# A graph-attention and mixture-of-experts layer: the experts' first product with its weights stationary, fetched per tile

## The chip, the cores and the metric

The kernel runs on one core of one Trainium2 chip. The metric is the device time of one execution in microseconds (us). Three executions of the kernel before took 1750.05, 1750.25 and 1754.41 us; the median is 1750.25 us.

## The reference

`x` holds 8192 tokens of 128 float32 values, `adj` an 8192 x 8192 int32 adjacency matrix. The layer is two residual steps:

```python
x = x + gnn(layernorm(x), adj, W, b_W, a_vec, b_a)      # masked attention over the graph
x = x + ffn(layernorm(x)[None], gate_w, gate_b, w1, w2, w3)[0]

def ffn(x, ...):                                         # 16 experts, hidden width 256
    top_probs, top_idx = top_k(softmax(x @ gate_w + gate_b), 2)      # then normalised to sum 1
    h1 = einsum('bsd,edh->bseh', x, w1); h2 = einsum('bsd,edh->bseh', x, w2)
    expert_out = einsum('bseh,eho->bseo', silu(h1) * h2, w3)
    return einsum('bseo,bse->bso', expert_out, dispatch)
```

The first step needs all 8192 x 8192 scores. In the second each token goes to two of 16 experts, so 16384 rows pass through a product 128 to 512 (w1 and w2 side by side), silu times gate, and a product 256 to 128.

## The kernel before

**Graph attention, 0 to about 1409 us.** Nine blocks of target rows (4 or 8 tiles of 128 rows) run over 64 tiles of source rows each. The SP queue streams the adjacency matrix into a ring of five staging buffers (`load_half`, L418 to L425), each load waiting for ScalarE's `sign` to have used the buffer. TensorE turns masks (L975) and accumulates the attention product (L990), VectorE makes logits (L1270), ScalarE exponentials (L779). While a block runs, the block before is normalised and routed, and GpSimd scatters its rows by indirect DMA to `xd_d`, a table in DRAM sorted by expert (`scatter`, L622 to L636: eight scatters for the first choice, a wait until all of them have landed, an iota on L619, eight for the second choice).

**Between the stages.** The last block is normalised and routed alone, a table `tab` of 144 tiles (first row and expert of each) is made, and the last rows are scattered. All of `w1` and `w2` (4 MB) has been loaded into one SBUF tile `w12` during the last block (L449 to L452).

**Experts, about 1436 to 1708 us.** 144 tiles of 128 rows, all of one expert each. I call the work of TensorE between two `m_h` a step. For tile i:

- SP loads the 128 rows, 130 words each (`load_tile`, L459 to L462), into `xs`, eight slots. The load of tile i waits on `y_out` until the result of tile i-8 has been written (L483), because its slot holds that tile's destinations and gate weight.
- `t_x` (L1063): TensorE transposes the rows into PSUM; ScalarE copies them to `xsT` (L871).
- `m_h` (L1067): one product with the rows as stationary operand and the expert's 512 columns of `w12` as moving operand. The expert's number is a register, read from `tab` by `expert_of` (L1058).
- ScalarE makes silu (L877), VectorE multiplies with the gate half (`do_hid`, L1527).
- `t_h` (L1073): two transposes of the 256 hidden columns; VectorE copies them to `hidT` (`copy_hT`, L1534).
- `m_y` (L1080): two accumulating products with `w3s`; ScalarE copies with the gate weight as scale (L883) into `ys`, four slots.
- GpSimd scatters the tile to `res_d` by indirect DMA (L698 to L702), which signals `y_out` when it lands.

TensorE's order is written out by hand: in step i come `m_h(i)`, `expert_of(i+1)`, `t_x(i+1)`, `t_h(i-1)`, `m_y(i-2)` (L1094 to L1128), with the first and the last eight tiles unrolled and a hardware loop of eight tiles in between. SP has a loop of eight tiles too (L480 to L484), at whose head one instruction loads eight registers of row numbers (`rows_of`). A float32 product of 128 rows is issued as two instructions, each with its own weight load (LDWEIGHTS); a transpose is one.

After the first eight row loads SP issues one load of 4 MB, `xm` (L479), for the last stage, which gathers the two results of every token, adds and stores (L487 to L496, L1545 to L1553).

Of the kernel before, what the change touches and what calls it, by code (L numbers as in the profile page):

```python
# [16 lines left out]
P = 128  # L17
# [23 lines left out]
def graph_moe_layer(nc, x, adj, W, b_W, a_vec, b_a, gate_w, gate_b, w1, w2, w3, out):  # L41
# [21 lines left out]
    SU = 4  # L63
    XS = 8
    GR = 8

# [38 lines left out]
    s1_d = nc.dram_tensor("s1_d", (NT, P), F32, kind="Internal").ap()  # L105
    xd_d = nc.dram_tensor("xd_d", (E * CAP + E * P, RW), F32, kind="Internal").ap()
    res_d = nc.dram_tensor("res_d", (2 * N + 2 * E * P, D), F32, kind="Internal").ap()

    with ExitStack() as ctx:
# [3 lines left out]
        def sem(name):  # L113
            return ctx.enter_context(nc.semaphore(name))
# [130 lines left out]
        xm, _ = carve(rA, 0, NT, D)  # L245
        w12, _ = carve(rB, 0, E, 2 * HID)
        w3s, _ = carve(urow[:, :].bitcast(F32), 0, E, HC * D)
# [5 lines left out]
        silu, at = carve(prf, at, 2, HID)  # L253
        hid, at = carve(prf, at, 2, HID)
        xsT, at = carve(prf, at, 2, D)
        hidT, at = carve(prf, at, 2, HID)
        ys, at = carve(prf, at, SU, D)
# [112 lines left out]
        tchain = sem("tchain")  # L370
        xs_in = [sem(f"xs_in{i}") for i in range(XS)]
        xsT_done = sem("xsT_done")
# [4 lines left out]
        hT_done = sem("hT_done")  # L377
        hT_ready = sem("hT_ready")
        y_done = sem("y_done")
# [34 lines left out]
        def _(sp):  # L414
# [3 lines left out]
            def load_half(b, i):  # L418
                c, k = pieces(b)[i // 2]
                n = 2 * PIECE0[b] + i  # L420
                if n >= STG:
                    sp.wait_ge(sign_done, n - STG + 1)
                r = (ROW0[b] + k) * P
                at = c * CH + i % 2 * HC2
                sp.dma_start(stage[:, n % STG, :], adj[r:r + P, at:at + HC2]).then_inc(adj_in[n % STG], 16)  # L425

            def load_s1(b):
# [30 lines left out]

            def load_tile(u, r, done):  # L459
                if done:  # L460
                    sp.wait_ge(y_out[u % SU], 16 * done)
# [7 lines left out]
            sp.wait_ge(tab_ready, 1)  # L469
            r = rows_of(0, XS)  # L470
            for c in range(2):
                sp.wait_ge(disp[c], 16 * NT)
            sp.wait_ge(pad_out, 16 * E)
            for u in range(XS):
                load_tile(u, r[u], 0)
            sp.wait_ge(xmid_out, 16 * LAST)
# [433 lines left out]
        def _(pe):  # L910
# [162 lines left out]
            def t_h(i, u):  # L1073
                pe.wait_ge(hid_ready, i + 1)
                for c in range(HC):
                    t = pe.transpose(bank[4 + u % 2][:, c * P:(c + 1) * P], hid[:, u % 2, c * P:(c + 1) * P],  # L1076
                                     identf[:, :])
                t.then_inc(hT_done, 1)

            def m_y(i, u, e, first):  # L1080
                pe.wait_ge(hT_ready, i + 1)
                if not first:
                    pe.wait_ge(y_ready, i - 1)
                for c in range(HC):
                    m = pe.matmul(bank[6 + u % 2][:, 0:D], hidT[:, u % 2, c * P:(c + 1) * P],  # L1085
                                  w3s[:, bass.ds(e, 1), c * D:(c + 1) * D].rearrange("p a b -> p (a b)"),
                                  start=(c == 0), stop=(c == HC - 1))
                m.then_inc(y_done, 1)


            pe.wait_ge(w12_in, 32)
            e = {0: expert_of(0)}
            t_x(0, 0, 1)
            for i in range(XS):  # L1094
                m_h(i, i, e[i])
                if i + 1 < XS:
                    e[i + 1] = expert_of(i + 1)
                t_x(i + 1, (i + 1) % XS, (i + 1) // XS + 1)
                if i >= 1:
                    t_h(i - 1, i - 1)  # L1100
                if i >= 2:
                    m_y(i - 2, i - 2, e[i - 2], i - 2 < 2)
            with pe.Fori(1, ST // XS - 1) as g:
                e = {0: expert_of(XS * g)}
# [11 lines left out]
            e = {first: expert_of(first)}  # L1116
            for i in range(first, ST + 2):
                if i < ST:
                    m_h(i, i % XS, e[i])
                    if i - 2 < first:  # L1120
                        e[i - 2] = expert_of(i - 2)
                    if i + 1 < ST:
                        e[i + 1] = expert_of(i + 1)
                if i + 1 < ST:
                    t_x(i + 1, (i + 1) % XS, (i + 1) // XS + 1)
                if i - 1 < ST:
                    t_h(i - 1, (i - 1) % XS)
                m_y(i - 2, (i - 2) % XS, e[i - 2], False)  # L1128

        @block.vector  # L1130
        def _(dve):
# [390 lines left out]

            def do_hid(i, v, first):
                dve.wait_ge(silu_ready, i + 1)
                if not first:
                    dve.wait_ge(hT_done, i - 1)
# [3 lines left out]
            def copy_hT(i, v, first):  # L1530
                dve.wait_ge(hT_done, i + 1)
                if not first:
                    dve.wait_ge(y_done, i - 1)
                dve.tensor_copy(hidT[:, v, :], bank[4 + v][:, 0:HID]).then_inc(hT_ready, 1)  # L1534

            do_hid(0, 0, True)
            copy_hT(0, 0, True)
            do_hid(1, 1, True)
            copy_hT(1, 1, True)
            with dve.Fori(1, ST // 2) as g:  # L1540
                for v in range(2):
                    do_hid(2 * g + v, v, False)
                    copy_hT(2 * g + v, v, False)

# [30 lines left out]
```

## Time and profile before

| | us |
|---|---|
| median of the three executions | 1750.25 |
| the profiled execution, own time | 1744.61 |
| its span | 1742.8 |
| experts' stage, first row load issued to last scatter | 1435.9 to 1705.2 |
| TensorE busy in the span | 1524.1 (87%) |
| VectorE, ScalarE, GpSimd busy | 1429.4, 1330.3, 495.5 |

Times in rows are microseconds from the start of the span. A timeline row gives start, duration, engine, line, instruction, tiles, count, and in brackets how long the engine was idle before it and what it waited for. PEld is TensorE's weight load, PEldq and SPq are the instruction streams of TensorE and SyncE, POOL is GpSimd, DVE VectorE and ACT ScalarE. A row "x4" merges four instructions: its start is the first one's start, its duration reaches to the end of the last.

### The profile page before, as it was taken

What the parts mean: (1) busy time and instruction counts of PE and PEld (TensorE: products, weight loads), DVE (VectorE), ACT (ScalarE), POOL (GpSimd) and SP (SyncE); (2) the same over time, 40 slices, a digit from 0 to 9 for tenths busy, and PEclk for the clock granted to TensorE, in tenths of its full rate; (3) what the DMA queues carried; (4) which work ended last, traced back from release to release, by engine and by line L of the source; (5) the groups of instructions that cost most, each with busy time, mean ns of one, the idle gap of its engine ahead of it and who ended that gap; (6) DMA issues with size and microseconds to landing.
All of it is one profiled execution on the core that took longest, in us unless ns stands there. A gap on an engine that the chain in (4) does not pass through costs nothing.

```text
span 1742.8 us, 24899 instructions
## 1 busy us (share of the span) xinstructions
PE 1524.1 (87%) x8110; PEld 837.4 (48%) x8111; DVE 1429.4 (82%) x1896; ACT 1330.3 (76%) x1804; POOL 495.5 (28%) x716
## 2 busy tenths in 40 slices
PE   5687899899989989998999899989999939999991
PEld 5554354454444444444444444445554515666660
DVE  6899999989998998999899989997895743444444
ACT  4899899889979987998798889977785624545550
POOL 6500001120314032403411260313025254555551
PEclk9999999999999999999999999999999979999996
DMA  7889687648847774886488657845523334222227
GB/s 244 298 303 316 219 283 251 218 160 262 258 145 245 236 261 136 261 256 233 139 268 259 203 175 260 265 139 159 157 73 104 111 69 159 72 71 73 75 73 298
DMA packets 127715, 339.40 MB, mean 195 GB/s; under 512 B 16962, under 2 KB 48898, under 8 KB 127490
## 3 DMA queue, kind: packets, MB, share of 16 engines
q1 hardware_dynamic: 106208, 304.06, 54.1%
q0 software_dynamic: 17056, 27.17, 5.8%
q10 hardware_dynamic: 4354, 6.92, 1.2%
q8 instruction: 56, 0.92, 0.2%
q14 instruction: 41, 0.34, 0.1%
HBM read 309.57 MB, written 28.51 MB: 194 GB/s over the span
## 4 chain that ended last, share of the span: by engine, by line
PE 39%; DVE 37%; issue 17%; ACT 3%; DMA 3%; POOL 2%; another core or an unknown queue 0%; SPq 0%; ACTq 0%; DVEq 0%; POOLq 0%
PE pair L990 18%; DVE probs L1270 17%; DVE ring L1238 16%; PE pair L1069 8%; PE pair L975 5%; PE pair L1085 4%; PE pair L1076 2%; ACT ring L728 1%; POOL X L536 1%; DMA ring<-res_d 1%; PE pair L1065 1%; DVE part L1238 1%; ACT probs L779 1%; PE pair L935 1%; DMA res_d<-probs 1%
## 5 line engine op out<-in xcount | busy, mean ns | idle before, releaser
L990 PE MATMUL pair<-probs,X 128*128 128x512 f32 x2048 | 1010.7, 611 | 1.9 <-ACT probs L779 1.8
L779 ACT ACTIVATE probs<-probs,ebias 128x1024 f32<-128x1024 f32 (+1 forms) x576 | 601.0, 1046 | 185.8 <-DVE probs L1270 179.4
L1270 DVE SCALAR_TENSOR_TENSOR probs<-s1row,ns,pair 128x1024 f32<-128x1024 f32 (+1 forms) x576 | 653.9, 1157 | 85.5 <-PE pair L975 73.0
L1238 DVE CUSTOM_DVE_ANT_0 ring<-urow,ring 128x2048 int8<-128x2048 f16 x256 | 585.0, 2289 | 5.7 <-ACT urow L747 4.9
L728 ACT ACTIVATE ring<-stage,neghalf 128x1024 int8<-128x1024 int32 x512 | 574.3, 1138 | 0.0
L975 PEld LDWEIGHTS pair<-diag,ring 128*128 128x128 fp8e5 x4096 | 262.4, 99 | 461.5 <-DVE probs L1270 258.2
L990 PEld LDWEIGHTS pair<-probs,X 128*128 128x128 f32 x2048 | 346.1, 192 | 219.3 <-issue 215.1
L975 PE MATMUL pair<-diag,ring 128*128 128x128 bf16 x4096 | 326.6, 220 | 117.2 <-DVE probs L1270 101.5
L700 POOL DMA_INDIRECT res_d<-probs x144 | 139.6, 969 | 133.6 <-ACT probs L883 125.7
L1534 DVE COPY probs<-pair 128x256 f32<-128x256 f32 x144 | 61.2, 425 | 139.6 <-PE pair L1076 89.6
L634 POOL DMA_INDIRECT xd_d<-xres,sloti x120 | 154.6, 1288 | 38.6 <-issue 31.6
L1069 PE MATMUL pair<-ring,probs 128*128 x288 | 158.6, 633 | 7.4 <-issue 4.1
L871 ACT ACTIVATE probs<-pair 128x128 f32<-128x128 f32 x144 | 40.0, 278 | 126.3 <-PE pair L1065 106.9
L576 POOL DMA_DIRECT2D xres<-in_x x7 | 11.7, 1672 | 358.6 <-ACT xres L821 358.6
L553 POOL TENSOR_SCALAR mrow<-rmax,kS,kB 128x8 f32<-128x8 f32 (+1 forms) x9 | 3.1, 350 | 379.4 <-DVE rmax L1246 379.4
L1085 PE MATMUL pair<-urow,probs 128*128 x576 | 89.1, 277 | 0.1
L1527 DVE TENSOR_TENSOR probs<-probs,pair 128x256 f32<-128x256 f32 x144 | 60.7, 421 | 19.0 <-ACT probs L877 15.8
L1085 PEld LDWEIGHTS pair<-urow,probs 128*128 128x128 f32 x576 | 75.6, 191 | 1.0 <-issue 0.3
L883 ACT ACTIVATE probs<-pair,probs 128x128 f32<-128x128 f32 x144 | 53.1, 369 | 23.1 <-PE pair L1085 6.9
L1076 PE MATMUL pair<-identf,probs 128*128 128x128 f32 x288 | 55.3, 274 | 0.4 <-ACT probs L883 0.4
L877 ACT ACTIVATE probs<-pair 128x256 f32<-128x256 f32 x144 | 54.4, 378 | 0.6 <-PE pair L1069 0.6
L1065 PE MATMUL pair<-identf,probs 128*128 128x128 f32 x144 | 41.1, 286 | 13.1 <-DMA probs<-xd_d 12.5
(239 smaller groups left out, 768.8 us busy)
## 6 DMA issues: line engine op xcount, KB each, us to landing
stage<-in_adj SPq DMA_DIRECT2D x512, 512.0 KB
probs<-xd_d SPq DMA_DIRECT2D x144, 65.0 KB
ring<-res_d SPq DMA_DIRECT2D x16, 512.0 KB, 9.8
ring<-in_L_ffn_w SPq DMA_DIRECT2D x2, 2048.0 KB, 11.8
ring<-xmid_d SPq DMA_DIRECT2D x1, 4096.0 KB
out<-ring ACTq DMA_DIRECT2D x8, 512.0 KB, 7.0
s1row<-s_d SPq DMA_DIRECT2D x7, 512.0 KB, 6.4
xres<-in_x POOLq DMA_DIRECT2D x7, 512.0 KB, 14.1
```

Source lines behind the costliest of these rows:

```text
L634: pool.indirect_dma_start(out=xd_d[:, :], out_offset=bass.IndirectOffsetOnAxis(ap=sloti[:, q, c, k:k + 1], axis=0), in_=xres[:, q, k, :], ...
L700: pool.indirect_dma_start(out=res_d[:, :], out_offset=bass.IndirectOffsetOnAxis(ap=xsI[:, i % XS, D:D + 1], axis=0), in_=ys[:, i % SU, :], ...
L728: act.activation(mask(b, c, k)[:, h:h + HC2], stage[:, n % STG, :], ACT.Sign, bias=neghalf[:, 0:1], scale=1.0).then_inc(sign_done, 1)
L779: act.activation(probs[:, n % PR, 0:wide], probs[:, n % PR, 0:wide], ACT.Exp, bias=ebias[:, j:j + 1], scale=RISE).then_inc(probs_ready, 1)
L975: t = pe.matmul(Tp[n % 2][:, k * P:(k + 1) * P], mask8(b, j, k), diag[:, q, k, :], start=True, stop=True)
L990: m = pe.matmul(acc[q][:, lo:hi], X[:, j, :], probs[:, n % PR, lo:hi], start=(j == 0), stop=(j == NT - 1))
L1069: pe.matmul(bank[2 + u % 2], xsT[:, u % 2, :], w12[:, bass.ds(e, 1), :].rearrange("p a b -> p (a b)"), start=True, stop=True).then_inc(h_d ...
L1076: t = pe.transpose(bank[4 + u % 2][:, c * P:(c + 1) * P], hid[:, u % 2, c * P:(c + 1) * P], identf[:, :])
L1085: m = pe.matmul(bank[6 + u % 2][:, 0:D], hidT[:, u % 2, c * P:(c + 1) * P], w3s[:, bass.ds(e, 1), c * D:(c + 1) * D].rearrange("p a b -> p ...
L1238: dve.tensor_tensor_reduce(m, urow[:, c * CH:(c + 1) * CH], m, CODE, NO_EDGE, ALU.subtract, ALU.max, part[:, k, c:c + 1]).then_inc(piece_d ...
L1270: dve.scalar_tensor_tensor(out=probs[:, n % PR, 0:wide], in0=s1row[:, q, 0:wide], scalar=ns2[:, j:j + 1], in1=Tp[n % 2][:, 0:wide], op0=AL ...
L1534: dve.tensor_copy(hidT[:, v, :], bank[4 + v][:, 0:HID]).then_inc(hT_ready, 1)
```

## The change

The first product of the experts is turned round: the weights are the stationary operand, in four blocks of 128 columns, and the transposed rows are the moving one, so the hidden values come out transposed. `t_h`, `copy_hT`, the tile `hid` and two semaphores go; `do_hid` writes `hidT` directly, which has four slots instead of two. `w12` no longer lies in SBUF as a whole: `w1` and `w2` are copied side by side into a DRAM tensor `w12_d` by 32 DRAM to DRAM transfers of 128 KB, issued by SP in blocks 2 to 5, and for each tile SP fetches its expert's 256 KB into one of eight slots `wt`. TensorE transposes rows two tiles ahead, so that step i is `m_h(i)`, `expert_of(i-1)`, `t_x(i+2)`, `m_y(i-2)`. The core of the diff:

```diff
+        wt, _ = carve(rB, 0, WS, 2 * HID)
-            sp.wait_ge(trans_done, used_up(GALL - 3))
-            w12v = w12.rearrange("p e (k h) -> p e k h", k=2)
-            sp.dma_start(w12v[:, :, 0, :], w1.rearrange("e d h -> d e h")).then_inc(w12_in, 16)
-            sp.dma_start(w12v[:, :, 1, :], w2.rearrange("e d h -> d e h")).then_inc(w12_in, 16)
+            def pair_weights(n):
+                e, k = divmod(n, 2)
+                sp.dma_start(w12_d[e, :, k * HID:(k + 1) * HID], (w1, w2)[k][e, :, :]).then_inc(w12_in, 16)
...
+                    if 2 <= b < 6 and i % 8 == 4:
+                        pair_weights(8 * (b - 2) + i // 8)
...
+            def load_weights(u, e):
+                sp.dma_start(wt[:, u, :], w12_d[bass.ds(e, 1), :, :].rearrange("a d h -> d (a h)")
+                             ).then_inc(wt_in[u], 16)
...
             for u in range(XS):
-                load_tile(u, r[u], 0)
+                load_tile(u, r[u])
+                load_weights(u, e[u])
...
             with sp.Fori(1, ST // XS) as g:
                 r = rows_of(XS * g, XS)
+                e = experts_of(XS * g, XS)
                 for u in range(XS):
+                    sp.wait_ge(h_done, XS * g + (u - XS + 1))
+                    load_weights(u, e[u])
                     sp.wait_ge(y_out[u % SU], 32 * g + (16 * (u // SU) - 16))
-                    load_tile(u, r[u], 0)
+                    load_tile(u, r[u])
...
-            def m_h(i, u, e):
+            def m_h(i, u, w, uses):
                 pe.wait_ge(xsT_ready, i + 1)
-                pe.matmul(bank[2 + u % 2], xsT[:, u % 2, :],
-                          w12[:, bass.ds(e, 1), :].rearrange("p a b -> p (a b)"), start=True, stop=True
-                          ).then_inc(h_done, 1)
+                pe.wait_ge(wt_in[w], 16 * uses)
+                for c in range(2 * HC):
+                    m = pe.matmul(bank[2 + u % 2][:, c * P:(c + 1) * P], wt[:, w, c * P:(c + 1) * P], xsT[:, u % 2, :],
+                                  start=True, stop=True)
+                m.then_inc(h_done, 1)
...
+            def free_h(i):
+                pe.wait_ge(hid_ready, i - 1)
...
                 for u in range(XS):
                     i = XS * g + u
-                    m_h(i, u, e[u])
-                    if u < 2:
-                        e[u - 2] = expert_of(XS * g + (u - 2))
-                    if u + 1 < XS:
-                        e[u + 1] = expert_of(XS * g + (u + 1))
-                    t_x(i + 1, (u + 1) % XS, g + 1 if u + 1 < XS else g + 2)
-                    t_h(i - 1, (u - 1) % XS)
+                    free_h(i)
+                    m_h(i, u, u, g + 1)
+                    if u == 0:
+                        e[-2] = expert_of(XS * g + -2)
+                    e[u - 1] = expert_of(XS * g + (u - 1))
+                    t_x(i + 2, (u + 2) % XS, g + 1 if u + 2 < XS else g + 2)
                     m_y(i - 2, (u - 2) % XS, e[u - 2], False)
...
-                dve.tensor_tensor(hid[:, v, :], silu[:, v, :], bank[2 + v][:, HID:2 * HID], ALU.mult
+                    dve.wait_ge(y_done, i - (HB - 1))
+                dve.tensor_tensor(hidT[:, w, :], silu[:, v, :], bank[2 + v][:, HID:2 * HID], ALU.mult
                                   ).then_inc(hid_ready, 1)
```

## Rows read from the trace of the kernel before

**Rows 1.** The page, its chain that ended last, shares of the span by line

```profile
PE pair L990 18%; DVE probs L1270 17%; DVE ring L1238 16%; PE pair L1069 8%; PE pair L975 5%; PE pair L1085 4%; PE pair L1076 2%; ACT ring L728 1%; POOL X L536 1%; DMA ring<-res_d 1%; PE pair L1065 1%; DVE part L1238 1%; ACT probs L779 1%; PE pair L935 1%; DMA res_d<-probs 1%
```

**Rows 2.** By stretch: length, busy PE, PEld, DVE, ACT, POOL; clock, DMA share, GB/s

```profile
1370.00:1374.00 4.00, 4.00 (x24) 2.17 (x23) 2.44 (x5) 2.66 (x4) 3.35 (x11) 1.00 1.10 359
1448.00:1452.00 4.00, 4.00 (x24) 2.94 (x23) 2.13 (x6) 2.33 (x9) 2.41 (x3) 1.00 0.97 412
...
1600.00:1640.00 40.00, 39.00 (x204) 25.50 (x203) 17.99 (x45) 20.50 (x68) 21.64 (x23) 1.00 0.27 73
```

**Rows 3.** Timeline of TensorE, one step of the experts' stage

```profile
1446.65 1.09 PE L1069 MATMUL pair<-ring,probs 128*128 x2
1447.58 0.27 PE L1065 MATMUL pair<-identf,probs 128*128 128x128 f32 x1
1447.69 0.38 PE L1076 MATMUL pair<-identf,probs 128*128 128x128 f32 x2
1447.90 0.61 PE L1085 MATMUL pair<-urow,probs 128*128 x4
1448.35 1.09 PE L1069 MATMUL pair<-ring,probs 128*128 x2
```

**Rows 4.** Timeline of TensorE, `m_h` of tile 8 and of tile 143, the last

```profile
1457.15 1.12 PE L1069 MATMUL pair<-ring,probs 128*128 x2
...
1700.52 1.09 PE L1069 MATMUL pair<-ring,probs 128*128 x2
```

**Rows 5.** TensorE's instruction stream by line, 1590 to 1633: ns min/median/max

```profile
L1059 PEldq TENSOR_LOAD <-stage x30: 295/300/429, 1590.4 to 1632.1; - x30
L1083 PEldq EVENT_SEMAPHORE  x18: 51/51/51, 1592.6 to 1630.0; - x18
```

**Rows 6.** Timeline of TensorE, eight pairs of weight load and matmul, then the next

```profile
800.84 0.62 PE L975 MATMUL pair<-diag,ring 128*128 128x128 bf16 x8
801.30 1.94 PE L990 MATMUL pair<-probs,X 128*128 128x512 f32 x4
```

**Rows 7.** Timeline: scatters on GpSimd, row loads on SP, around loop heads

```profile
1449.20 0.97 POOL L700 DMA_INDIRECT res_d<-probs  x1 [0.73 <-ACT probs L883]
1605.66 0.98 POOL L700 DMA_INDIRECT res_d<-probs  x1 [1.63 <-ACT probs L883]
...
1595.31 0.33 SPq L462 DMA_DIRECT2D probs<-xd_d  x1
1597.07 0.33 SPq L462 DMA_DIRECT2D probs<-xd_d  x1
1608.06 0.33 SPq L462 DMA_DIRECT2D probs<-xd_d  x1
```

**Rows 8.** SP's instruction stream, 1590 to 1640, one load of eight registers: ns, first start

```profile
L455 SPq TENSOR_LOAD <-stage x4: 558/572/595, 1596.0 to 1639.1; - x4
```

**Rows 9.** Timeline of the stage's start: SP's issues, and `t_x` of tile 8

```profile
1435.87 4.37 SPq L462 DMA_DIRECT2D probs<-xd_d  x8
1440.36 0.36 SPq L479 DMA_DIRECT2D ring<-xmid_d  x1
1454.15 6.27 SPq L462 DMA_DIRECT2D probs<-xd_d  x6
1456.01 0.33 PE L1065 MATMUL pair<-identf,probs 128*128 128x128 f32 x1 [1.48 <-DMA probs<-xd_d]
```

**Rows 10.** Timeline in a block: 512 KB loads, last scatter, iota that waits for it

```profile
853.60 0.33 SPq L425 DMA_DIRECT2D stage<-in_adj  x1
854.63 0.33 SPq L425 DMA_DIRECT2D stage<-in_adj  x1
...
854.83 0.96 POOL L634 DMA_INDIRECT xd_d<-xres,sloti  x1 [0.30 <-issue]
859.26 0.15 POOL L619 IOTA xres<- 128x8 int32 x1 [3.47 <-DMA xd_d<-xres,sloti]
```

**Rows 11.** The page, costliest groups: busy, mean ns, then idle before

```profile
L728 ACT ACTIVATE ring<-stage,neghalf 128x1024 int8<-128x1024 int32 x512 | 574.3, 1138 | 0.0
```

More of the change, by code:

```diff
@@ L64, in graph_moe_layer @@
     XS = 8
+    WS = 8
+    HB = 4
     GR = 8
@@ L106, in graph_moe_layer @@
     xd_d = nc.dram_tensor("xd_d", (E * CAP + E * P, RW), F32, kind="Internal").ap()
+    w12_d = nc.dram_tensor("w12_d", (E, D, 2 * HID), F32, kind="Internal").ap()
     res_d = nc.dram_tensor("res_d", (2 * N + 2 * E * P, D), F32, kind="Internal").ap()
@@ L245, in graph_moe_layer @@
         xm, _ = carve(rA, 0, NT, D)
-        w12, _ = carve(rB, 0, E, 2 * HID)
+        wt, _ = carve(rB, 0, WS, 2 * HID)
         w3s, _ = carve(urow[:, :].bitcast(F32), 0, E, HC * D)
@@ L253, in graph_moe_layer @@
         silu, at = carve(prf, at, 2, HID)
-        hid, at = carve(prf, at, 2, HID)
         xsT, at = carve(prf, at, 2, D)
-        hidT, at = carve(prf, at, 2, HID)
+        hidT, at = carve(prf, at, HB, HID)
         ys, at = carve(prf, at, SU, D)
@@ L371, in graph_moe_layer @@
         xs_in = [sem(f"xs_in{i}") for i in range(XS)]
+        wt_in = [sem(f"wt_in{i}") for i in range(WS)]
         xsT_done = sem("xsT_done")
@@ L376, in graph_moe_layer @@
         hid_ready = sem("hid_ready")
-        hT_done = sem("hT_done")
-        hT_ready = sem("hT_ready")
         y_done = sem("y_done")
@@ L457, in rows_of, with experts_of, load_tile @@
                     skip_runtime_bounds_check_because="the first row of a tile in an expert's part of the dispatch")[1]
-            def load_tile(u, r, done):
-                if done:
-                    sp.wait_ge(y_out[u % SU], 16 * done)
+            def experts_of(i, n):
+                return nc.values_load_multi_w_load_instructions(
+                    tab[0:1, bass.ds(ST + i, n)], engines=(mybir.EngineType.SP,), min_val=0, max_val=E - 1,
+                    skip_runtime_bounds_check_because="every tile of the table belongs to one of the experts")[1]
+            def load_tile(u, r):
                 sp.dma_start(xs[:, u, :], xd_d[bass.ds(r, P), :]).then_inc(xs_in[u], 16)
+            def load_weights(u, e):
+                sp.dma_start(wt[:, u, :], w12_d[bass.ds(e, 1), :, :].rearrange("a d h -> d (a h)")
+                             ).then_inc(wt_in[u], 16)
             sp.wait_ge(proj_read, ROUND0[NB])
@@ L470, in _ @@
             r = rows_of(0, XS)
+            e = experts_of(0, XS)
             for c in range(2):
@@ L473, in _ @@
             sp.wait_ge(pad_out, 16 * E)
+            sp.wait_ge(w12_in, 16 * 2 * E)
             for u in range(XS):
-                load_tile(u, r[u], 0)
+                load_tile(u, r[u])
+                load_weights(u, e[u])
             sp.wait_ge(xmid_out, 16 * LAST)
@@ L1065, in t_x, with m_y @@
                 pe.transpose(bank[u % 2][:, 0:P], xs[:, u, 0:D], identf[:, :]).then_inc(xsT_done, 1)
-            def m_h(i, u, e):
+            def m_h(i, u, w, uses):
                 pe.wait_ge(xsT_ready, i + 1)
-                pe.matmul(bank[2 + u % 2], xsT[:, u % 2, :],
-                          w12[:, bass.ds(e, 1), :].rearrange("p a b -> p (a b)"), start=True, stop=True
-                          ).then_inc(h_done, 1)
-            def t_h(i, u):
-                pe.wait_ge(hid_ready, i + 1)
[L1075 to L1081, printed above, removed]
+                pe.wait_ge(wt_in[w], 16 * uses)
[3 more added lines that the diff above has]
+                m.then_inc(h_done, 1)
+            def m_y(i, u, e, first):
+                pe.wait_ge(hid_ready, i + 1)
                 if not first:
@@ L1084, in m_y @@
                 for c in range(HC):
-                    m = pe.matmul(bank[6 + u % 2][:, 0:D], hidT[:, u % 2, c * P:(c + 1) * P],
+                    m = pe.matmul(bank[6 + u % 2][:, 0:D], hidT[:, u % HB, c * P:(c + 1) * P],
                                   w3s[:, bass.ds(e, 1), c * D:(c + 1) * D].rearrange("p a b -> p (a b)"),
@@ L1088, in m_y @@
                 m.then_inc(y_done, 1)
-            pe.wait_ge(w12_in, 32)
-            e = {0: expert_of(0)}
+            def free_h(i):
+                pe.wait_ge(hid_ready, i - 1)
+            e = {}
             t_x(0, 0, 1)
+            t_x(1, 1, 1)
             for i in range(XS):
[L1095 to L1098, printed above, removed]
+                if i >= 2:
+                    free_h(i)
+                m_h(i, i, i, 1)
                 if i >= 1:
-                    t_h(i - 1, i - 1)
+                    e[i - 1] = expert_of(i - 1)
+                t_x(i + 2, (i + 2) % XS, (i + 2) // XS + 1)
                 if i >= 2:
@@ L1103, in _ @@
             with pe.Fori(1, ST // XS - 1) as g:
-                e = {0: expert_of(XS * g)}
+                e = {}
                 for u in range(XS):
                     i = XS * g + u
-                    m_h(i, u, e[u])
-                    if u < 2:
-                        e[u - 2] = expert_of(XS * g + (u - 2))
-                    if u + 1 < XS:
-                        e[u + 1] = expert_of(XS * g + (u + 1))
-                    t_x(i + 1, (u + 1) % XS, g + 1 if u + 1 < XS else g + 2)
-                    t_h(i - 1, (u - 1) % XS)
+                    free_h(i)
+                    m_h(i, u, u, g + 1)
[3 more added lines that the diff above has]
+                    t_x(i + 2, (u + 2) % XS, g + 1 if u + 2 < XS else g + 2)
                     m_y(i - 2, (u - 2) % XS, e[u - 2], False)
             first = ST - XS
-            e = {first: expert_of(first)}
+            e = {}
             for i in range(first, ST + 2):
                 if i < ST:
[L1119 to L1125, printed above, removed]
+                    free_h(i)
+                    m_h(i, i % XS, i % WS, i // WS + 1)
+                if i == first:
+                    e[i - 2] = expert_of(i - 2)
                 if i - 1 < ST:
-                    t_h(i - 1, (i - 1) % XS)
+                    e[i - 1] = expert_of(i - 1)
+                if i + 2 < ST:
+                    t_x(i + 2, (i + 2) % XS, (i + 2) // XS + 1)
                 m_y(i - 2, (i - 2) % XS, e[i - 2], False)
@@ L1521, in _, with do_hid @@
             dve.tensor_copy(tab[0:1, :], bank[3][0:1, 0:2 * ST]).then_inc(tab_ready, 1)
-            def do_hid(i, v, first):
+            def do_hid(i, v, w, first):
                 dve.wait_ge(silu_ready, i + 1)
                 if not first:
-                    dve.wait_ge(hT_done, i - 1)
-                dve.tensor_tensor(hid[:, v, :], silu[:, v, :], bank[2 + v][:, HID:2 * HID], ALU.mult
+                    dve.wait_ge(y_done, i - (HB - 1))
+                dve.tensor_tensor(hidT[:, w, :], silu[:, v, :], bank[2 + v][:, HID:2 * HID], ALU.mult
                                   ).then_inc(hid_ready, 1)
[L1530 to L1543, printed above, removed]
+            for i in range(HB):
+                do_hid(i, i % 2, i, True)
+            with dve.Fori(1, ST // HB) as g:
+                for w in range(HB):
+                    do_hid(HB * g + w, w % 2, w, False)
             dve.wait_ge(xm_in, 16)
```

## The prediction

> **What bounds the kernel now.** I read the chain that ended last first: beside the attention's lines it holds L1069, L1085, L1076 and L1065, together 15% of the span [rows 1]. They are TensorE's products and transposes of the experts' stage, the part that the change rewrites. The busy times by stretch come second: in that stage TensorE is busy 39.0 of 40 us at the full clock (2.4 GHz), VectorE 18.0, ScalarE 20.5, GpSimd 21.6, and the DMA engines have a share of 0.27 [rows 2]. So the stage runs at TensorE's pace. The timeline gives the step: `m_h` 0.93 us, `t_x` 0.11, the two of `t_h` 0.21, `m_y` 0.45, in all 1.70 [rows 3]. From `m_h` of tile 8 to that of tile 143 it is 243.4 us, 1.803 for each of 135 steps [rows 4]; eight take 14.4, of which 0.8 is the head of the hardware loop.
>
> **TensorE's part.** A pair of a weight load and a 128-column matmul is passed every 0.11 us (`m_y`: four in 0.45; `t_h`: two in 0.21) [rows 3]. The new `m_h` is four blocks of two such pairs: 8 x 0.1125 = 0.90 for 0.93, so turning the product round costs nothing, and `t_h` is gone. The new step is 13 pairs, 1.46 us. The instruction stream has to keep up: 26 instructions at no more than 0.029 (eight pairs in 0.46 [rows 6]) are 0.75, the register load of `expert_of` 0.30, and six waits and three register operations, all taken like the wait of 0.051 [rows 5], 0.45. That is 1.50, and I take it; the bounds are 1.46 and 1.56. At the loop head I keep 0.8; its lower bound is 0.5, one register load less. TensorE alone would go at (8 x 1.50 + 0.8) / 8 = 1.60.
>
> Here a rule speaks against the change. The trace shows four pairs on `m_y` in 0.45 us, each with a weight load of its own [rows 3], so loads pass beside the matmul before. The Trainium skill (TensorE: Matmul & The Clock Gate, The mechanism) says that a weight load overlaps a running matmul only if it goes to another row group, which full 128-row loads never do; by it no load would be hidden.
>
> **What the removed work was worth elsewhere.** `copy_hT` leaves VectorE, which was idle half the time: nothing. The load of `w12` ran while TensorE was busy 4.00 of 4.00 us [rows 2]: nothing. The 32 copies in DRAM come between adjacency loads for which ScalarE never sat idle [rows 11]: nothing; with that cover gone it would be 8 MB of traffic at 359 GB/s [rows 2], 23 us. `free_h` waits for a product that VectorE ends some 1 us after its `m_h`, two steps ahead: nothing. The weights of tile i are issued before its rows and used two steps after `t_x(i)`, and 256 KB at 412 GB/s [rows 2] are 0.64 us: never late.
>
> **The loop that was slack.** The rows of tile j+8 are loaded once the scatter of tile j has landed. From such a load's issue to the transpose is 1.86 us (1454.15 to 1456.01 [rows 9]); from `m_y` to the scatter's start 1.30 (1447.90 to 1449.20 [rows 3, 7]); from there to SP's next load 2.40 (1605.66 to 1608.06 [rows 7]). Before, `t_x(j+8)` comes five steps after `m_y(j)`: with `t_x` and `t_h` between, 5.88 us against 8.5, nobody waits. Now it comes four steps after: 0.11 + 1.30 + 2.40 + 1.86 = 5.67 against 4 x 1.50 = 6.0. The slack is nearly gone, by the transpose moved one tile ahead and by the shorter step.
>
> And SP becomes late once in eight tiles. Its registers for eight tiles load 0.7 us after the last row load of the group was issued and take 0.57 [rows 7, 8]; now a second such load follows (0.6), then the weights' issue (0.56, as eight issues and the next took 4.49 [rows 9]), and about 0.1 of waits and registers on either side: the row load of tile 8g comes 2.55 us after that of 8g-1, where a step is 1.5. So there is a closed chain from one group to the next: rows of 8g land 1.86; three steps of TensorE over the loop head 3 x 1.50 + 0.8 = 5.3; `t_x`, `m_y`, scatter, landing 3.81, which releases the rows of 8g+7; SP to the rows of 8g+8 2.55. The sum is 13.52 for eight tiles, more than TensorE's 12.8: 1.69 a step.
>
> **Contention.** The trace has no stage with scatters beside 256 KB bursts, so I bound it. Below: nothing. Above, the nearest row: in a block two loads of 512 KB were issued around a scatter, and it landed after 4.43 us for 2.40 [rows 10, 7], 2.0 us late, where the 1 MB takes 2.6 at 404 to 412 GB/s: a scatter loses at most what the bytes beside it take. That is 0.64 for the scatter and 0.64 for the rows behind the weights in SP's queue, 1.3 in the chain. In steady order the bursts mostly fall between the scatters, and SP issues the two 0.56 apart; I take 0.5. The chain is 14.02, 1.753 a step, and 135 steps are 236.6: 6.8 us less.
>
> The Trainium skill (DMA: Bandwidth & Descriptors, Latency and other measured facts) gives the memory 0.2 us of latency on average and 2 at high load. By that the two transfers in the chain could be 3.6 longer, an estimate from that page, and the kernel would take about 1801.
>
> **The start.** SP issues the 4 MB `xm` after the first loads, and the scatter of tile 0 lands only once `xm` is through; then tile 8 is loaded, at 1454.15 [rows 9]. Eight more issues put `xm` 8 x 0.56 = 4.5 us later; half a weight transfer behind it adds 0.3. `t_x(8)` moves from 1456.0 to 1460.8. It now belongs to step 6, so `m_y` and one whole step follow: 0.11 + 0.45 + 1.50, `m_h(8)` at 1462.9 for 1457.15: 5.7 us more. Bounds: 3.5 and 8. After the last `m_h` nothing of weight changes.
>
> **Sum.** -6.8 + 5.7 = -1.1 us. The profiled execution took 1744.61 (span 1742.8), 5.6 under the median of 1750.25; so it would take 1743.5, and the median 1749.2.
>
> **The rivals.**
>
> Faster: the chain through SP does not close. The two register loads overlap (0.6 less) and the bursts miss the scatters (0.2 left): 13.1 for eight tiles, 1.64 a step, 22.0 less, and with the start 16.3 less: 1734. For it: nothing reads the second eight registers before the weights' issue, and before the change the head of SP's loop was hidden. Against it: a register load takes 0.57 and SP's stream is in order. It decides under 13.78 us per eight tiles.
>
> Slower: every burst delays the next scatter and the next rows by its whole 0.64. The chain is 14.8, 1.853 a step, 6.7 more, with the start 12.4 more: 1763. For it: the loaded scatter lost three quarters of the time of the bytes beside it [rows 10], and 256 KB more each step put the DMA share at 0.28 + 0.64 / 1.8, about 0.65. It decides above 14.4 us, a contention of 0.9. At the top of the start's bound it would be 1765, with a step of 1.56 on TensorE 1768.
>
> The turned product is not cheap: no weight load is hidden. A load is 25.5 us for 203 [rows 2], 0.13 each, so a step is 13 x (0.13 + 0.11) = 3.1 us, 175 more: 1931. That is what the rule on row groups would do; the rows of `m_y` refute it unless more than four pairs in a row differ.
>
> **Chances.** 0.3% of 1750 is 5.3 us, about what a measurement can tell. The chain as I price it, 13.78 to 14.4: 0.38, its own range 1744.9 to 1755.5. Faster: 0.33, most of it in 1733 to 1745. Slower: 0.28, to 1768. Exposed weight loads: 0.01. The range of 1733 to 1768 leaves out about 2 in 10 (a chain under 13.1; contention above 1.3).
>
> **What would show it.** In the changed profile: `m_h` starts to `t_x` 0.9 us with eight matmuls; TensorE idle before L1065 (`t_x`) for DMA, about 1 us once in eight tiles; SP's row load of 8g some 2.5 us after the one before; scatter start to SP's next row load 2.4 to 3.0; a step of 1.75 on average; `m_h(8)` near 1463; VectorE some 60 us less busy; the DMA share 0.6 to 0.7. The prediction is wrong if TensorE is idle before `t_x` in every step (contention), if it never is (the chain does not close), or if ScalarE now sits idle before L728.

## The result and the profile after

The changed kernel takes 1781.65 us (1776.60 to 1782.63, four runs) where the kernel before takes 1750.15 (medians). The ratio of the mean times is 1.0168, with a 95% interval of 1.0143 to 1.0194. It is slower by 31 us, outside the range of the prediction. The profiled execution has a span of 1779.0 us for 1742.8.

The busy times by stretch (columns as in [rows 2]), first the attention stage of the kernel before, then the changed kernel:

```profile
0.00:1400.00 1400.00, 1257.03 (x6765) 666.27 (x6767) 1275.61 (x1515) 1189.24 (x1357) 338.11 (x552) 1.00 0.68 215
...
0.00:1400.00 1400.00, 1256.32 (x6771) 666.84 (x6773) 1275.91 (x1516) 1189.91 (x1357) 331.45 (x553) 1.00 0.68 215
...
1560.00:1600.00 40.00, 34.63 (x259) 30.65 (x259) 8.38 (x20) 18.43 (x60) 19.47 (x21) 1.00 0.70 198
1600.00:1640.00 40.00, 35.02 (x263) 30.85 (x262) 8.25 (x21) 18.44 (x60) 19.15 (x20) 1.00 0.68 196
```

TensorE is now busy 35.0 of 40 us where it was 39.0 [rows 2], and the DMA share went from 0.27 to 0.68. The attention stage did not move: its busy times are those of before within 7 us (GpSimd) and 1 us (the others), ScalarE still never waits for an adjacency load (idle before L746, the `sign`, is 0.0 us, as in [rows 11]), and the experts' first row load is issued at 1436.54 for 1435.87. The page's rows of `t_x`, before and after (busy, mean ns, then idle before it), show TensorE waiting for rows:

```profile
L1065 PE MATMUL pair<-identf,probs 128*128 128x128 f32 x144 | 41.1, 286 | 13.1 <-DMA probs<-xd_d 12.5
L1083 PE MATMUL pair<-identf,probs 128*128 128x128 f32 x144 | 45.7, 317 | 58.2 <-DMA probs<-xd_d 49.3
```

What stopped TensorE stands in its timeline, here with SP's issues and GpSimd's scatters (L1083 is `t_x`, L1090 `m_h`, L1099 `m_y`, L718 the scatter, L470 SP's row load, L473 its weight load; other rows are left out):

```profile
1601.43 0.33 PE L1083 MATMUL pair<-identf,probs 128*128 128x128 f32 x1
1602.17 1.06 PE L1090 MATMUL pair<-probs,ring 128*128 128x128 f32 x8
1603.02 0.97 POOL L718 DMA_INDIRECT res_d<-probs  x1 [0.98 <-ACT probs L901]
1603.07 0.27 PE L1083 MATMUL pair<-identf,probs 128*128 128x128 f32 x1
1603.16 0.33 SPq L470 DMA_DIRECT2D probs<-xd_d  x1
1603.62 1.06 PE L1090 MATMUL pair<-probs,ring 128*128 128x128 f32 x8
1605.40 0.33 PE L1083 MATMUL pair<-identf,probs 128*128 128x128 f32 x1 [0.73 <-DMA probs<-xd_d]
1606.15 1.06 PE L1090 MATMUL pair<-probs,ring 128*128 128x128 f32 x8
1606.20 0.33 SPq L470 DMA_DIRECT2D probs<-xd_d  x1
```

Where nothing stops it, a step is 1.45 us (`m_h` at 1602.17 and 1603.62), but 115 of the 119 steps from `t_x` to `t_x` up to tile 142 are longer than 1.5. Here the row load issued at 1603.16 lands for a `t_x` at 1605.40, 2.24 us later, and TensorE stood idle for it. The scatter of 1603.02 releases the row load of 1606.20, 3.18 us later. From `m_h` of tile 8 (1464.22) to that of tile 143 (1735.37) it is 271.2 us, 2.01 a step, for 1.80 before [rows 4].

The chain that ended last says the same by line, first before (1460 to 1690), then after (1480 to 1700):

```profile
by line: PE pair L1069 52.2%; PE pair L1085 24.7%; PE pair L1076 12.0%; PE pair L1065 8.8%; issue 2.2%; ACT probs L871 0.2%
...
by line: DMA res_d<-probs 22.5%; DMA probs<-xd_d 21.1%; issue 17.5%; PE pair L1090 9.7%; PE pair L1099 8.9%; SPq L470 4.6%; PE pair L1083 4.5%; SPq L473 4.3%; ACT probs L901 2.6%; SPq L465 1.6%; SPq L460 1.1%; SPq L495 0.6%; POOL res_d L718
```

Before, the chain was TensorE's products. Now its first two lines are the scatter to DRAM and the rows from there. I call them the two ways: the scatter's way runs from a scatter's start to the row load that it releases, the rows' way from a row load to its `t_x`. I took both for each of 120 tiles (row loads of tiles 24 to 143) from the starts in the timeline. The scatter's way has a median of 3.52 us, least 2.59, the rows' way 2.90, least 1.86. The quiet values, against which I count contention below, are the prediction's 2.40 and 1.86. For the scatter's way the trace before has a median of 2.42. For the rows' way it has no median to compare, since there the rows mostly lie ready before TensorE wants them: 1.86 is the one load for which `t_x` waited [rows 9]. SP was already waiting when the scatter landed for 97 of the 120 row loads, so the scatter's way is in the main DMA and not SP's lateness.

### The profile page after: what moved, and what is told of

Read it like the earlier page. It is cut to its first block, busy times and chain, and to the rows that moved or that the text cites. A ratio compares the mean times of both kernels' runs of the same rounds, so it can differ in the third digit from the quotient of the medians.

```text
span 1779.0 us, 26224 instructions
## 1 busy us (share of the span) xinstructions
PE 1518.1 (85%) x8686; PEld 895.0 (50%) x8687; DVE 1372.6 (77%) x1752; ACT 1330.5 (75%) x1804; POOL 487.4 (27%) x716
## 4 chain that ended last, share of the span: by engine, by line
DVE 36%; PE 29%; issue 19%; DMA 10%; SPq 2%; POOL 2%; ACT 1%; ACTq 0%; another core or an unknown queue 0%; POOLq 0%; DVEq 0%
PE pair L1008 18%; DVE probs L1286 17%; DVE ring L1254 16%; PE pair L993 5%; DMA res_d<-probs 4%; DMA probs<-xd_d 4%; PE pair L1090 2%; PE pair L1099 2%; POOL X L554 1%; DMA ring<-res_d 1%; PE pair L1083 1%; DVE part L1254 1%; SPq L470 1%; SPq L473 1%; PE pair L953 1%
## 5 line engine op out<-in xcount | busy, mean ns | idle before, releaser
L746 ACT ACTIVATE ring<-stage,neghalf 128x1024 int8<-128x1024 int32 x512 | 574.2, 1138 | 0.0
L718 POOL DMA_INDIRECT res_d<-probs x144 | 139.2, 966 | 171.1 <-ACT probs L901 157.9
L1090 PE MATMUL pair<-probs,ring 128*128 128x128 f32 x1152 | 156.0, 279 | 1.8 <-issue 0.2
L652 POOL DMA_INDIRECT xd_d<-xres,sloti x120 | 146.2, 1218 | 38.7 <-issue 31.7
L1090 PEld LDWEIGHTS pair<-probs,ring 128*128 128x128 f32 x1152 | 142.4, 194 | 4.8 <-issue 4.5
L1099 PE MATMUL pair<-urow,probs 128*128 x576 | 98.7, 294 | 1.5 <-ACT probs L901 1.5
L1083 PE MATMUL pair<-identf,probs 128*128 128x128 f32 x144 | 45.7, 317 | 58.2 <-DMA probs<-xd_d 49.3
L1099 PEld LDWEIGHTS pair<-urow,probs 128*128 128x128 f32 x576 | 75.5, 191 | 8.5 <-issue 1.6
L1083 PEld LDWEIGHTS pair<-identf,probs 128*128 128x128 f32 x144 | 20.4, 142 | 77.4 <-DMA probs<-xd_d 52.2
```

Source lines behind the costliest of these rows:

```text
L652: pool.indirect_dma_start(out=xd_d[:, :], out_offset=bass.IndirectOffsetOnAxis(ap=sloti[:, q, c, k:k + 1], axis=0), in_=xres[:, q, k, :], ...
L718: pool.indirect_dma_start(out=res_d[:, :], out_offset=bass.IndirectOffsetOnAxis(ap=xsI[:, i % XS, D:D + 1], axis=0), in_=ys[:, i % SU, :], ...
L746: act.activation(mask(b, c, k)[:, h:h + HC2], stage[:, n % STG, :], ACT.Sign, bias=neghalf[:, 0:1], scale=1.0).then_inc(sign_done, 1)
L1083: pe.transpose(bank[u % 2][:, 0:P], xs[:, u, 0:D], identf[:, :]).then_inc(xsT_done, 1)
L1090: m = pe.matmul(bank[2 + u % 2][:, c * P:(c + 1) * P], wt[:, w, c * P:(c + 1) * P], xsT[:, u % 2, :], start=True, stop=True)
L1099: m = pe.matmul(bank[6 + u % 2][:, 0:D], hidT[:, u % HB, c * P:(c + 1) * P], w3s[:, bass.ds(e, 1), c * D:(c + 1) * D].rearrange("p a b -> ...
```

## The experiments

The kernels of a group ran on one chip, and the kernel before ran beside them: it took 1733.22 us beside the first group, 1744.06 beside the second and 1732.24 beside the third. So all times are compared as ratios to the kernel before on the same chip. The diffs show the lines that matter; "..." stands for what is left out. "Step" is the mean distance of `t_x` from tile 24 to 142; it is 1.81 us in the kernel before and 2.02 in the changed one.

**First group: what is it?** e1 takes the traffic away:

```diff
                 for u in range(XS):
-                    sp.wait_ge(h_done, XS * g + (u - XS + 1))
-                    load_weights(u, e[u])
                     sp.wait_ge(y_out[u % SU], 32 * g + (16 * (u // SU) - 16))
...
-                    m_h(i, u, u, g + 1)
+                    m_h(i, u, u, 1)
```

> The changed kernel without the 136 weight loads inside SP's loop; the register loads of experts stay, every tile after the eighth uses the weights of the first eight tiles (the hidden values are those of wrong experts). Theory (the row loop): a row load waits for the scatter eight tiles back and is needed four steps after m_y; the loop is 5.67 us of latency plus what the weight traffic adds, about 2.2. Without the traffic 5.67 / 4 = 1.42 falls below TensorE's 1.60, so the step goes from 2.0 to about 1.6 and the kernel to about 1727. Rival A (SP's lateness at the group head carries it): the second register load stays, so no more than 0.6 us in eight tiles comes back, 10 us: about 1771. Rival B (13 pairs and their instruction stream cost more than 1.5 on TensorE): no change, 1782.

Measured: 0.9849 (0.9822 to 0.9876), 1709.6 us, step 1.56. The chip is another than the one I expected a time for; by ratio it is 56 us below the change. The computation turned round is fast; the traffic, with what waits for it and SP's work to issue it, is the whole loss. Rivals A and B fall. This run also has the quiet ways in steady work, as the median time from issue to landing; below it the same lines of g0, the changed kernel taken once more in the third group:

```profile
probs<-xd_d SPq DMA_DIRECT2D x115, 65.0 KB, 1.8
res_d<-probs POOLq DMA_INDIRECT x116, 2.3
...
probs<-xd_d SPq DMA_DIRECT2D x91, 65.0 KB, 3.0
res_d<-probs POOLq DMA_INDIRECT x91, 3.4
```

e3 keeps the traffic and gives the rows more slots:

```diff
-    XS = 8
+    XS = 16
...
-        xs, at = carve(prf, at, XS, RW)
+        xs, at = carve(rB, at, XS, RW)
...
+                    for v in range(WS):
+                        u = WS * half + v
+                        sp.wait_ge(h_done, XS * g + (u + 1))
+                        load_weights(v, e[v])
+                        sp.wait_ge(y_out[u % SU], 64 * g + (16 * (u // SU) + 16))
+                        load_tile(u, r[v])
```

> The changed kernel with sixteen slots for rows instead of eight (they move into the free half of the ring region behind the weight slots), weights still eight slots and the same traffic. Theory (row loop): the loop now spans twelve steps, so contention of 2 us in it is hidden, TensorE sets the step at about 1.6, the kernel takes 1730 to 1740. Rival (the traffic itself is the bound, through the weight transfers or the result slots): the step stays near 2.0 and the kernel near 1780.

Measured: 0.9906 (0.9878 to 0.9934), 1717.9 us, step 1.63. With the same bytes moving and the rows needed twelve steps after `m_y` instead of four, the loss turns into a gain. The waits of e3 in 1490 to 1660 show what is left (engine, line, whom it waited for, us in total, times, longest): TensorE no longer waits for rows but for weights.

```profile
PE pair L1099 <- DMA ring<-w_d: 9.0, 16, 1.4
PEld pair L1099 <- DMA ring<-w_d: 8.3, 11, 1.6
```

e4 does the traffic alone, in the kernel before:

```diff
                 for u in range(XS):
+                    sp.wait_ge(h_done, XS * g + (u - XS + 1))
+                    sp.wait_ge(dum_in[u], 16 * g + 16)
+                    sp.dma_start(dum[:, u, :], x_4[u * P:(u + 1) * P, :]).then_inc(dum_in[u], 16)
                     sp.wait_ge(y_out[u % SU], 32 * g + (16 * (u // SU) - 16))
...
```

> The kernel before with nothing changed but 136 transfers of 256 KB from DRAM to unused SBUF slots, issued by SP just where the change issues the weights. Theory (row loop): contention adds 2 us to the loop, 5.88 + 2.2 = 8.1 us against five steps of 1.70 (8.5): nearly hidden, plus SP's later issue at the group head; 1750 to 1757. Rival (the traffic costs as such, whatever the lead): about 1780 as with the change. The traces also give the contention alone: scatter start to the next row load 2.4 before, about 3.5 here.

Measured: 1.0017 (1.0003 to 1.0031), 1737.2 us, step 1.80. The contention is all there: the median of the scatter's way is 3.56 us for 2.40. It costs 3 us in the whole kernel by ratio, since the loop has five steps of 1.7.

e5 takes the change's other part back:

```diff
-                    t_x(i + 2, (u + 2) % XS, g + 1 if u + 2 < XS else g + 2)
+                    t_x(i + 1, (u + 1) % XS, g + 1 if u + 1 < XS else g + 2)
```

> The changed kernel with rows transposed one tile ahead again (t_x(i+1) in step i), all else as changed. The loop then spans five steps, 7.9 / 5 = 1.58, but each m_h has to wait for ScalarE's copy of a transpose that ended 0.45 us before: 0.3 to 0.4 of idle per step, 1.85 with the loop head. Theory (row loop): about 1760. Rival A (SP or traffic as such): 1782 or more, since nothing of theirs changed and the wait comes on top.

Measured: 0.9995 (0.9981 to 1.0009), 1732.5 us, step 1.74. One step more in the loop is worth what the change lost, though `m_h` now waits for the copy of the rows. I had priced that wait at 0.3 to 0.4 in each step; most steps are 1.64, so it is 0.2 over the undisturbed 1.45.

**Second group: do the causes add, and what sets the contention?** The two parts go into the kernel before, f3 with rows transposed two tiles ahead, f4 with that and e4's traffic:

```diff
-                    t_x(i + 1, (u + 1) % XS, g + 1 if u + 1 < XS else g + 2)
+                    t_x(i + 2, (u + 2) % XS, g + 1 if u + 2 < XS else g + 2)
```

> The kernel before with one thing changed: rows are transposed two tiles ahead (t_x(i+2) in step i), as the change does. The row loop then spans four steps of 1.70: 6.8 us for 5.88 needed. Theory (row loop): still slack, the time is that of before within 3 us. Rival (the order of TensorE's work itself costs): slower by more than 5 us.

> The kernel before with both: rows transposed two tiles ahead, and the 136 unused transfers of 256 KB. Theory (row loop): 5.88 + 2.2 = 8.1 us over four steps is 2.0 a step for 1.80: 25 to 30 us slower than before, though the traffic alone cost 3 us and the transpose ahead alone costs none. Rival (the causes add): about 3 us slower than before.

Measured: f3 0.9981 (0.9967 to 0.9995), f4 1.0161 (1.0143 to 1.0180), steps 1.74 and 1.93. With e4, which ran on the chip of the first group, this makes a table of two causes:

| kernel before, ratio | no traffic | 256 KB a tile |
|---|---|---|
| rows one tile ahead (loop of five steps) | 1 | 1.0017 |
| rows two tiles ahead (loop of four) | 0.9981 | 1.0161 |

Alone, the traffic costs 0.2% and the order gains 0.2%; both together cost nearly what the change costs (1.0168). They don't add; they meet in one loop.

f2 asks for SP's lateness at the head of its loop:

```diff
-                e = experts_of(XS * g, XS)
...
-                    load_weights(u, e[u])
+                    sp.dma_start(wt[:, u, :], w12_d[u, :, :]).then_inc(wt_in[u], 16)
```

> The changed kernel with the same weight traffic, but from fixed experts, so that SP's loop has no second load of eight registers (wrong experts' weights from tile 8 on). Theory (row loop with contention in every step): SP's row load at the group head comes 0.6 us earlier, which matters once in eight tiles: 0 to 10 us less than the change. Rival (SP's lateness at the head is what binds, as the chain of the prediction had it): the whole 0.6 per group comes back, 10 us, and the step without it falls to 1.9 or less.

Measured: 1.0158 (1.0139 to 1.0177), step 1.93. SP's row load at the head came 2.19 us after the one before (median) for 2.75 in the change, so the lateness was shortened as meant, and the stage gives back 0.06 to 0.09 a step (against g0 and the change), some 10 us, at the upper end of my expectation. By whole times it is less: 1.0158 lies within the interval of the change's own 1.0168 on the first chip and outside that of the repeat below, 1.0198 (1.0180 to 1.0216). So the second register load costs something between nothing and 12 us of the 31; these runs do not fix it better. My test did not separate theory and rival well, as both allowed 10 us; the step of 1.93 is above the 1.9 that the rival wanted.

f1 halves the bytes of each weight load, the number of descriptors stays:

```diff
+            def load_half_weights(u, e):
+                sp.dma_start(wt[:, u, 0:HID], w12_d[bass.ds(e, 1), :, 0:HID].rearrange("a d h -> d (a h)")
+                             ).then_inc(wt_in[u], 16)
...
-                    load_weights(u, e[u])
+                    load_half_weights(u, e[u])
```

> The changed kernel, but each weight load inside SP's loop brings only w1's half of an expert, 128 KB in rows of 1 KB, as many descriptors as before (the gate half of the hidden values is then that of a wrong expert). Theory A (the bytes beside a transfer delay it): the contention of about 2.2 us in the loop of four steps halves, 5.67 + 1.1 over 4 is 1.7, the step goes from 2.0 to 1.7 and the kernel loses 35 to 40 us against the change. Theory B (each transfer delays the others by a fixed time, whatever its size): the step stays at 1.95 to 2.0, within 8 us of the change.

Measured: 1.0061 (1.0044 to 1.0078), 1755.0 us, step 1.82; the scatter's way is 2.93 us, the rows' 2.29. Of the change's 1.12 and 1.04 us of contention 0.53 and 0.43 are left, a little under half. The bytes count, as A says, but the time fell less than I expected, about 19 us by ratio where I had 35 to 40. The steps tell why. Seven of eight are 1.68 us on average, as the plain loop gives (the two ways and the rest are 5.22 + 1.41 = 6.6 us, 1.66 a step). The eighth, which ends with `t_x` of a tile 8g, is 2.81: SP issues that tile's row load 3.10 us after the one before (median). The chain of the prediction through SP's head gives 13.52 + 0.96 = 14.5 us for eight tiles, 1.81 a step, which is the 1.82 measured, and SP came too late to wait for the landing in 50 of 120 row loads, for 23 in the change. So with the contention halved it is that chain that closes. In the change itself the eighth step is 2.35 and the others 1.97.

**Third group.** g0 is the changed kernel, unedited:

> The changed kernel as it is, once more on this chip, so that the three beside it can be compared with it directly: about 1.017 of the kernel before, step 2.0.

Measured: 1.0198 (1.0180 to 1.0216), 1765.8 us, step 1.99, the two ways 3.50 and 2.84: the loss is there on a second chip, and a little larger. This trace tells for 30 of the 120 tiles when their rows landed: `t_x` starts 0.04 or 0.05 us later in 24 of them and at most 0.26 later in five more, so TensorE did wait for nearly every tile.

g3 moves the same bytes as 64 rows of 4 KB:

```diff
-                    load_weights(u, e[u])
+                    sp.dma_start(wt[0:64, u, :], w12_d[bass.ds(e[u], 1), :, :].rearrange("a (d q) h -> d (a q h)", q=2)
+                                 ).then_inc(wt_in[u], 16)
```

> The changed kernel with the in-loop weight loads of the same 256 KB laid out as 64 rows of 4 KB instead of 128 of 2 KB (the weights then lie wrongly; the product of all tiles after the eighth is that of stale weights). In f1 half the bytes in the same number of descriptors halved the contention: a scatter lost 0.5 us instead of 1.1. Theory A (the bytes count): the same 2.0 a step, 1.017. Theory B (the 2 KB rows move below the full rate, and it is the time that the engines are held that counts): contention falls towards 0.64 for each transfer, 1.75 to 1.85 a step, 15 to 30 us less than the change.

Measured: 1.0347 (1.0325 to 1.0369), 1791.3 us, step 2.15, the two ways 4.02 and 3.17. Neither theory had that sign: bytes alone do not explain it. But B's quantity, the time for which the engines are held, orders the three runs. The stretches of g3 and of f1 (columns as in [rows 2]):

```profile
1520.00:1560.00 40.00, 32.20 (x238) 28.43 (x239) 7.40 (x18) 16.86 (x54) 17.47 (x19) 1.00 0.75 182
```

```profile
1520.00:1560.00 40.00, 36.76 (x286) 33.43 (x285) 9.54 (x23) 19.84 (x69) 20.42 (x22) 1.00 0.51 146
```

Share times step, less the 0.27 x 1.80 = 0.49 us that rows and results take [rows 2, 4], is the time for which one tile's weights hold all engines. It is an estimate: the shares differ by some 0.03 between stretches of one run, which is 0.1 us.

| | share x step - 0.49 | scatter's way over 2.40 | rows' way over 1.86 |
|---|---|---|---|
| f1, 128 rows of 1 KB | 0.51 x 1.82: 0.44 | 0.53 | 0.43 |
| the change, 128 of 2 KB | 0.68 x 2.01: 0.88 | 1.12 | 1.04 |
| g3, 64 of 4 KB | 0.75 x 2.15: 1.12 | 1.62 | 1.31 |

The delay goes with the time held, at 1.0 to 1.5 of it. Three points that differ in more than one thing do not prove a law, and why 64 longer rows are slower than 128 was not tried.

g1 and g2 follow the waits of e3. g1 is e3 with the load `xm` cut into pieces; g2 is g1 with SP loading rows twelve tiles ahead in its sixteen slots. The second diff is against g1:

```diff
             with sp.Fori(0, ST // XS - 1) as g:
+                sp.dma_start(xm[:, bass.ds(GR * g, GR), :], xm_src[:, bass.ds(GR * g, GR), :]).then_inc(xm_in, 16)
...
```

> Sixteen row slots (as in e3) and the 4 MB load xm cut into eight loads of 512 KB, one every sixteen tiles in SP's loop. Theory: in e3 TensorE stood still for 13 us after tile 9, because the scatter of tile 0, which the result slots wait for, lands only behind xm; with the pieces that stop goes, the pieces cost 1.3 us each of DMA time and mostly hide: 8 to 12 us less than e3's ratio of 0.9906, about 0.985. Rival (the stop has another cause, or the pieces stop the stage eight times): no better than 0.99.

```diff
                         load_weights(v, e[v])
-                        sp.wait_ge(y_out[u % SU], 64 * g + (16 * (u // SU) + 16))
-                        load_tile(u, r[v])
+                        if u >= 4 or not peeled:
+                            sp.wait_ge(y_out[u % SU], 64 * g + 16 * (u // SU))
+                        load_tile((u + 12) % XS, r[v])
```

> g1 with one more edit: SP loads rows twelve tiles ahead instead of sixteen, still in sixteen slots, so it waits for a scatter twelve tiles back, which has long landed, and issues each tile's weights as soon as their slot is free. Theory: what is left in e3 (1.63 a step against 1.56 without traffic) is TensorE waiting for weights that SP issued late, behind its wait for the scatter; it goes: 1.58 a step, 5 to 8 us less than g1. Rival (the weights come late because the DMA engines are near full): as g1.

Measured: g1 0.9921 (0.9904 to 0.9937), step 1.68; g2 0.9720 (0.9698 to 0.9742), 1684.6 us, step 1.449. g1 alone gave nothing: the stop before `t_x` of tile 10 shrank from 13.4 to 5.3 us (distance to the `t_x` before it), but the pieces of 512 KB stand before the weights in SP's queue. TensorE waited 12.5 us for weights in 1490 to 1640, and the step right behind a piece, one in sixteen, takes 3.45 us on average where e3 has 2.30. g2 then gave 33 us where I had expected 5 to 8. Its stretch:

```profile
1520.00:1560.00 40.00, 40.00 (x361) 40.00 (x361) 11.38 (x27) 25.48 (x84) 27.35 (x29) 1.00 0.95 301
```

TensorE is busy 40 of 40 us while the DMA engines are at 0.95. In all 118 steps the distance is 1.449 or 1.450. The rival, that full DMA engines make the weights late, is refuted: the engines are fuller than in g1 (0.85) and the weights come in time, so SP had issued them late. This version beats both kernels, the one before by 2.8%, 48 us.

## Why the prediction was wrong

- **The step on TensorE.** Right in kind and too careful. I had 1.46 from the pairs, and took 1.50 for the instruction stream and 0.8 for the loop head, 1.60 together. g2 shows 1.449 including its loop heads, so both additions were nothing there. The rule that a weight load overlaps only a matmul on another row group (the Trainium skill, TensorE: Matmul & The Clock Gate, The mechanism) is contradicted: thirteen pairs in a row pass at 0.11 us each, with the rows of matmuls and of weight loads both busy 40.00 of 40.00 us at a granted clock of 1.00 (2.4 GHz).
- **The work taken off VectorE, the copies in DRAM, the weights' own lateness.** Right in the changed kernel: VectorE is busy 57 us less (1429.4 to 1372.6), and TensorE had not waited for that copy before (idle before L1085, `m_y`, 0.1 us). No wait for weights stands in the traces of the change, e5, f1, f2, g0 or g3. They came late only in e3 and g1, where SP waited for other things first.
- **The start.** `t_x(8)` was forecast at 1460.8 and came at 1460.73. `m_h(8)` was forecast at 1462.9 and came at 1464.22: 7.1 us later than before, for 5.7. The 1.4 us missed are TensorE's clock. It had stood idle for 10.14 us before `t_x(8)`, and the granted clock was 0.54 from 1460 to 1464, the lower of its two levels (1.2 GHz) for most of it; `m_h(7)` took 1.89 us for 1.06:

```profile
1460.00:1464.00 4.00, 3.27 (x16) 3.25 (x17) 0.00 (x0) 0.67 (x3) 0.97 (x1) 0.54 0.80 238
1464.00:1468.00 4.00, 4.00 (x38) 4.00 (x37) 1.26 (x3) 2.09 (x8) 1.93 (x2) 1.00 0.37 114
...
1460.73 0.48 PE L1083 MATMUL pair<-identf,probs 128*128 128x128 f32 x1 [10.14 <-DMA probs<-xd_d]
1461.01 1.15 PE L1099 MATMUL pair<-urow,probs 128*128 x4
1461.95 1.89 PE L1090 MATMUL pair<-probs,ring 128*128 128x128 f32 x8
```

- **The loop without contention.** The way and its length were right: 5.67 us over four steps, slack nearly gone. e1's landings (1.8 and 2.3 us) bear out the two ways. f3 shows the slack was still enough, f4 and e4 that the lead of five steps had been hiding the traffic.
- **Contention: the step that failed.** I bounded it by 1.3 us for the chain of eight tiles, 0.64 for each of two transfers, and took 0.5. It was 1.12 + 1.04 = 2.16 (medians), in nearly every loop of four steps, and TensorE idle before `t_x` in every step was one of my own signs of being wrong. Three things failed. The 0.64 came from 412 GB/s, the rate of `xm` with 32 KB per partition; the weights' 2 KB rows hold the engines for 0.88 us. I argued that the bursts fall between the scatters; the least of 120 scatter ways is 2.59, above the quiet 2.40, so none missed them here (in g0 the least is 2.44). And I counted one burst for each transfer, from [rows 10], as the most that it can lose. But a way of 3.5 us is longer than a step: between a scatter's start and its row load SP issues 1.6 weight loads on average, two in 69 of the 120. That this is why the loss is above the 0.88 of one burst is my reading; no run takes it apart.
- **Which chain closes.** With 2.16 in it the plain loop of four steps is 7.83 us, 1.96 a step, and binds nearly everywhere; my chain through SP's head, 13.52 + 2.16 = 15.7 for eight tiles, gives the same 1.96. What is left to 2.01, 7 us of 135 steps, lies nearly all outside the contention. By means, the four parts of the loop are 0.19 from `t_x` to `m_y`, 1.46 to the scatter, 3.57 and 2.87, 8.09 us or 2.02 a step, and the 0.19 and 1.46 were 0.11 and 1.30 in my sum. The chain through SP's head, to which I gave the most room, adds little in the change: the one step in eight that it lengthens is 0.38 above the others, 6 us in all, and f2 says the same within its spread. In f1 it closes.
- **The sum.** The 135 steps took 271.2 us where I had 236.6. Between profiled executions the miss is 1780.8 - 1743.5 = 37.3 us: 34.6 in these steps, 1.4 at the start and 1.3 behind the last `m_h`. Between medians it is 32.5, because the 5.6 us by which the profiled execution before lay under its median did not come again (0.9 after). The slower rival, which had 0.28 of the chances, named the right mechanism, every burst delaying the next scatter and the next rows, with its size at 60% of the true one (1.3 of 2.16), hence 1763. The estimate from the page on DMA (the Trainium skill, DMA: Bandwidth & Descriptors, Latency and other measured facts), was 3.6 us for the two transfers against 2.16 measured, and 1801 misses by 19 us on the other side.

## What to carry to other kernels

When a change adds steady traffic, look for every loop that goes through a DMA and back, count its steps and its latency, and see how much slack it has: a loop that hid everything before can be the bound after one order of instructions is moved. Price a transfer beside others by how long it holds the DMA engines at its own row length, not by the rate of the best transfer in the trace, and count how many such bursts pass while the other one is under way. A queue that waits for one slot before it issues for another turns a full buffer into a late load; ask for slots that have long been free, and let the wait be satisfied when it is reached.

## What was unexpected of the hardware

- 256 KB as 64 partitions of 4 KB held the DMA engines for 1.12 us, as 128 partitions of 2 KB for 0.88, and 128 KB as 128 of 1 KB for 0.44 (estimates, worked out above from share and step).
- TensorE ran thirteen float32 pairs of weight load and 128-column matmul a step at 1.449 us, over hardware loops of sixteen tiles with a register load of 0.3 us in every step, without losing any of it (g2: 40.00 of 40.00 us busy, weight loads too).
- With the DMA engines at a share of 0.95 and 301 GB/s the stage still ran at TensorE's pace (g2). Latency had been the limit of the change, not bandwidth.
